# Writing out the attention heads' loop, and storing split weights in longer rows

## What is computed

```python
x = L0_attn_x                                   # (1, 1024, 256)
xn = layernorm(x)
s = attention(xn, wq, wk, wv, wo, ...)          # 16 heads of 128; q and k are RMS-normed
g = silu(mixture_of_experts_0(xn, ...))         # 32 experts of width 128
x = x + s * g
xn = layernorm(x)
s = gated_linear_attention(xn, Wq, ..., W1, W3, W2)   # a recurrence, then a gated MLP
g = silu(mixture_of_experts_1(xn, ...))         # 64 experts of width 64
x = x + s * g
```

## Time and profile before

| | |
|---|---|
| Median of 3 runs | 1166.0 us (1164.7 to 1166.66) |
| Span of the profiled execution | 1166.5 us |
| PE (TensorE matmuls) busy | 1036.1 us, 89% |
| VectorE busy | 827.8 us, 71% |
| ScalarE busy | 622.8 us, 53% |
| POOL busy | 579.7 us, 50% |
| DMA packets | 196552, 122.42 MB |

### The profile page before, as it was taken

How to read it: one execution, slowest core, us unless ns; L and a number is a source line. 1 busy time by engine, 2 the same in 40 slices (tenths; PEclk the granted TensorE clock), 3 DMA queues, 4 the chain that set the end, 5 groups by cost and what they waited for, 6 DMA issues and landing times. The chain is left out here.

```text
span 1166.5 us, 23260 instructions
## 1 busy us (share of the span) xinstructions
PE 1036.1 (89%) x7790; PEld 689.9 (59%) x7790; DVE 827.8 (71%) x1461; ACT 622.8 (53%) x1225; POOL 579.7 (50%) x449
## 2 busy tenths in 40 slices
PE   5976979999999999699999999979987967979797
PEld 4465766666666666366666666647933425557544
DVE  3768347877887688478787778854569974866557
ACT  3555166667666666366666666742360115646532
POOL 3211557657765776366586556443218401631173
PEclk9965999999999999899999999989998989979899
DMA  5664023757674755736755765563011308659932
GB/s 173 113 198 133 1 55 64 63 102 81 97 64 101 76 96 70 103 41 84 86 89 82 79 96 74 73 94 110 1 68 77 126 12 253 209 164 299 309 91 90
DMA packets 196552, 122.42 MB, mean 105 GB/s; under 512 B 75044, under 2 KB 189782, under 8 KB 196182
## 3 DMA queue, kind: packets, MB, share of 16 engines
q1 hardware_dynamic: 178934, 97.74, 45.7%
q10 hardware_dynamic: 14432, 14.81, 3.8%
q0 software_dynamic: 3072, 8.39, 2.1%
HBM read 81.90 MB, written 36.37 MB: 101 GB/s over the span
## 5 line engine op out<-in xcount | busy, mean ns | idle before, releaser
L1309 DVE TENSOR_REDUCE a_nmax<-psum 128x1 f32<-128x1024 f32 x128 | 156.1, 1219 | 83.7 <-PE psum L1157 79.2
L1315 DVE SCALAR_TENSOR_TENSOR a_pT<-psum,a_pT 128x512 f16<-128x512 f32 x256 | 164.9, 684 | 25.9 <-ACT a_pT L1252 19.2
L1252 ACT ACTIVATE a_pT<-psum 128x512 f16<-128x512 f32 x256 | 140.4, 603 | 25.7 <-PE psum L1168 14.1
L1070 POOL TENSOR_TENSOR a_rnorm<-a_ss,a_power 128x8 f32<-128x8 f32 x32 | 58.4, 1824 | 182.0 <-DVE a_ss L1285 182.0
L1244 ACT ACTIVATE a_ex<-psum,a_nmax 128x1024 f32<-128x1024 f32 x128 | 142.6, 1114 | 11.4 <-PE psum L1168 10.6
L1168 PE MATMUL psum<-ident,a_ex 128*128 128x128 f32 x1024 | 134.4, 274 | 8.2 <-issue 7.9
L1168 PEld LDWEIGHTS psum<-ident,a_ex 128*128 128x128 f32 x1024 | 120.2, 141 | 26.5 <-DVE a_pT L1315 1.7
L1139 PE MATMUL psum<-a_wh,xT_h 128*128 128x128 f16 (+1 forms) x512 | 115.2, 248 | 2.0 <-PEq L2754 2.0
L1140 PE MATMUL psum<-a_wl,xT_h 128*128 128x128 f16 (+1 forms) x512 | 115.2, 248 | 0.0
L1141 PE MATMUL psum<-a_wh,xT_l 128*128 128x128 f16 (+1 forms) x512 | 115.0, 248 | 0.0
L1179 PE MATMUL psum<-a_pT,a_vh 128*128 128x512 f16 x256 | 98.1, 383 | 12.0 <-DVE a_of L988 11.0
(11 more groups left out here) (397 smaller groups left out, 2536.0 us busy)
## 6 DMA issues: line engine op xcount, KB each, us to landing
split_gate_up<-a_e_wh SPq DMA_DIRECT2D x64, 128.0 KB
a_rb<-row_scales SPq DMA_DIRECT2D x32, 256.0 KB, 4.0
g_e_gu<-split_gate_up SPq DMA_DIRECT2D x32, 256.0 KB, 3.7
block_outputs<-g_e_ym ACTq DMA_DIRECT2D x16, 512.0 KB, 4.9
split_rest<-a_e_wh SPq DMA_DIRECT2D x45, 128.0 KB
wf<-in_L_ffn_W_gate SPq DMA_DIRECT2D x32, 128.0 KB, 2.4
wf<-in_L_ffn_W_up SPq DMA_DIRECT2D x32, 128.0 KB, 2.5
wf<-in_L_ffn_W_down SPq DMA_DIRECT2D x32, 128.0 KB, 3.0
```

What stands on the lines that cost most here:

```text
L1252: act.activation(pT[g][:, 0, 4 * h:4 * h + 4, (m % 4) * P:(m % 4 + 1) * P], bank_of(r, unit).rearrange("p (k q) -> p k q", k=4), ACT.Copy, ...
L1309: dve.tensor_reduce(nmax[:, k:k + 1], score_banks(m), AX.X, ALU.max, negate=True).then_inc(max_ready, 1)
L1315: dve.scalar_tensor_tensor(low, bank_of(r, unit).rearrange("p (k q) -> p k q", k=4), PROB, high, ALU.mult, ALU.subtract).then_inc(low_done, 1)
```

## The change

- `heads` has no loop any more: all 16 heads are written out on TensorE, ScalarE and VectorE, and POOL's list is written out as well. The same instructions on tiles are issued in the same order; what a wait compares with is now a constant.
- In POOL's split the halves' buffer of an expert chunk is laid out as (block of 256 numbers, half, 256), so that high and low of a block lie side by side: 1 KB. The two instructions that write it (L822, L826) and the one between them (L824) have three-dimensional views. For the chunks of the rest the layout stays.
- `store` issues two DMAs for a chunk, not three: for expert chunks one with gate and up (256 rows of 1 KB) and one with down (128 rows of 1 KB), for the rest one for each half (128 rows of 1.5 KB each). Counts of the semaphore `stored` go from 48 to 32 a chunk. What lies in DRAM afterwards is the same as before, and so are its readers.

```diff
-        self.halves = [tmp(f"e1_wh{b}", [P, 2, self.WIDTH], F16) for b in range(2)]
+        halves = [tmp(f"e1_wh{b}", [P, 2 * self.WIDTH], F16) for b in range(2)]
+        self.blocks = [x[:, :].rearrange("p (i a d) -> p i a d", a=2, d=D) for x in halves]
+        self.parts = [x[:, :].rearrange("p (a c) -> p a c", a=2) for x in halves]
...
-        whole = self.wf[b][:, :]
-        lift = self.lift.to_broadcast([P, self.WIDTH])
-        high, low = self.halves[b][:, 0, :], self.halves[b][:, 1, :]
+        t, j = k // 3, k % 3
+        if j < 2:
+            whole = self.wf[b][:, :].rearrange("p (i d) -> p i d", d=D)
+            lift = self.lift.unsqueeze(2).to_broadcast([P, self.WIDTH // D, D])
+            high, low = (self.blocks[b][:, :, part, :] for part in range(2))
+        else:
+            whole = self.wf[b][:, :]
+            lift = self.lift.to_broadcast([P, self.WIDTH])
+            high, low = (self.parts[b][:, part, :] for part in range(2))
         pool.wait_ge(self.loaded[b], 16 * self.LOADS * uses)
-        if not (isinstance(uses, int) and uses == 1):
-            pool.wait_ge(self.stored[b], 48 * uses - 48)
+        if uses > 1:
+            pool.wait_ge(self.stored[b], 32 * uses - 32)
...
             two = slice(4 * t + 2 * j, 4 * t + 2 * j + 2)
+            sp.dma_start(self.gu[two, :, :, :].rearrange("e p a x -> p e (a x)"),
+                         self.blocks[b][:, 0:2, :, :].rearrange("p e a x -> p e (a x)")).then_inc(self.stored[b], 16)
+            sp.dma_start(self.dn[two, :, :, :].rearrange("e f a d -> (e f) (a d)"),
+                         self.blocks[b][:, 2, :, :].rearrange("p a d -> p (a d)")).then_inc(self.stored[b], 16)
+        else:
             for part in range(2):
-                sp.dma_start(self.gu[two, :, part, :].rearrange("e p x -> p e x"),
-                             self.halves[b][:, part, 0:2 * self.GU].rearrange("p (e x) -> p e x", e=2)).then_inc(self.stored[b], 16)
-            sp.dma_start(self.dn[two, :, :, :].rearrange("e f a d -> (e f) a d"), self.halves[b][:, :, 2 * self.GU:])\
-              .then_inc(self.stored[b], 16)
-        else:
-            for at in range(0, self.WIDTH, D):
-                sp.dma_start(self.rest[:, :, t * self.WIDTH + at:t * self.WIDTH + at + D], self.halves[b][:, :, at:at + D])\
+                sp.dma_start(self.rest[:, part, t * self.WIDTH:(t + 1) * self.WIDTH], self.parts[b][:, part, :])\
                   .then_inc(self.stored[b], 16)
...
-        def heads(engine, head):
-
-            head(0, 0)
-            head(1, 1)
-            with engine.Fori(0, 2) as i:
-                for r in range(2, 8):
-                    head(6 * i + r, r)
-            head(H - 2, H - 2)
-            head(H - 1, H - 1)
+        def heads(head):
+            for t in range(H):
+                head(t, t)
...
-                for t in range(2):
-                    past(t, 1 - t, t + 2, t % 2, 3 * t // 2 + 1)
-                with pool.Fori(0, (H - 6) // 2) as i:
-                    for b in range(2):
-                        past(2 * i + 2 + b, 1 - b, i + 3 + b, b, 3 * i + 4 + b)
-                for t in range(H - 4, H):
-                    past(t, 1, H // 2, t % 2, 3 * t // 2 + 1)
+                for t in range(H):
+                    past(t, (t + 3) % 2, (t + 3) // 2 + 1, t % 2, 3 * t // 2 + 1)
```

More of the change, by code:

```diff
@@ L851, in wait_stored @@
         for b, done in enumerate(self.stored):
-            sp.wait_ge(done, 48 * len(range(b, chunks, 2)))
+            sp.wait_ge(done, 32 * len(range(b, chunks, 2)))
 def attention0(nc, env, w):
@@ L1202, in _ @@
                 scores(0, 1, 0, None)
-                heads(pe, head)
+                heads(head)
                 for piece in range(4):
@@ L1271, in _ @@
                 exps(0, 0)
-                heads(act, head)
+                heads(head)
                 high_outputs(act, H - 1, 0)
@@ L1356, in _ @@
                 squares(1, 0, NS + 2)
-                heads(dve, head)
+                heads(head)
                 finished(dve, H - 1, 0)
```

## The result

| | before | after |
|---|---|---|
| Median (runs) | 1165.35 us (4: 1163.7 to 1166.66) | 1147.68 us (4: 1142.63 to 1151.09) |
| Ratio, 95% interval | | 0.9848, 0.9821 to 0.9875 |
| Span of the profiled execution | 1166.5 us | 1146.6 us |
| DMA packets | 196552 | 175819 |

The forecast was 1147.9 us. That it came so close is partly luck, as the account by stages shows: three terms were too small, and other stages and the step from the span to the median took their excess back.

A forecast was written before the change was run, and what follows sets the result against it. PE was taken as the bound, busy 89% of the span. The jump's 13.4 and register work's 4.7 us, 18.1 together, off the 1166.5 us span gave 1148.4, less 0.5 for the median 1147.9 us; range 1138 to 1154.

The forecast's parts named there:

- The jump: Head 8, where the loop jumps back: writing it out removes idle time and the low clock after it, 13.4 us.
- Rival (4): Stall at 480 to 489 us is DMA's and returns: about 1161 or 1166; 0.02 with no gain, 0.03 shared with one stop.
- the case of one new stop: Written-out list fetched late once, at the jump's price of 13.4 us: 1161.3; 0.03, shared with the DMA stall keeping part gain.
- The register work: Loop's heads: working out wait values in registers costs 0.39 us a head, for 12 heads 4.7 us, ends 2.0 and 8.8.
- the middle of 0.17 and 0.60: Register cost a head taken as 0.39 us, between the L1126 wait difference and all idle time above head 1's.
- POOL's split and the longer rows: POOL's three-dimensional views and SP's fewer stores in longer rows were taken to be worth nothing to PE.
- The stop in head 15 stays: Row load (14, 1) stays caught behind the slow row store; PE's 6.91 us idle remains, no gain counted.
- the limit of 769.4: Head 15's row load must issue by 769.4, 1.85 us earlier, but its earlier row store lands only then.
- Rival (1): The stop in head 15 goes too, giving back at most 7.6 us: 1140.3; chance 0.34.
- the last step of the sum: From span to median: the runs' median lies 0.5 below the span, so 1148.4 becomes 1147.9 us.
- Rival (3): Written-out list fetched late in heads 8 to 13, 13.4 us each time: 1174.7 from the second stop on, chance 0.04.
- Rival (2): Only the jump counts; the loop heads' 1.03 us idle has other causes: 1152.6, at worst 1155.6; chance 0.15.

The follow-up runs named there:

- hold_all: Kernel before, with SP's row store (7, 1), store of chunk 23 and load of chunk 25 held back until TensorE passed the jump; 1166.08 us in one run.
- loop_rows16: Kernel before, loop and weight stores kept, with row sums stored as 128 rows of 16 bytes and VectorE's strided read; 1149.02 us, ratio 0.9798.
- heads_out: Kernel before with only the loops written out on all four engines, stores still three a chunk in rows of 512 bytes; 1144.33 us, ratio 0.9861.
- after_third: The changed kernel unedited, measured a third time, on another chip; 1160.84 us, ratio 0.9888 to the kernel before.
- long_rows: Kernel before with the new longer-row stores and POOL's list written out; TensorE, ScalarE and VectorE keep their loop; 1162.89 us, ratio 1.0016.
- after_again: The changed kernel unedited, measured and profiled once more; 1144.84 us, ratio 0.9871 to the kernel before.
- hold_chunks: Kernel before, with SP's store of chunk 23 and load of chunk 25 held back until TensorE's first scores behind the jump; 1168.89 us in one run.
- hint_loop: Kernel before, with an instruction per loop turn announcing the jump back to the instruction fetch on TensorE, ScalarE and VectorE; 1171.06 us, ratio 1.0047.
- no_jump: Kernel before, its loop of two turns made two loops of one turn; register work vanished too on TensorE, ScalarE and VectorE; 1145.79 us, ratio 0.9878.
- rows16: The changed kernel with inverse row sums stored as 128 rows of 16 bytes, not 512 numbers of 4, and VectorE's strided read; 1143.57 us, ratio 0.9795.
- rows16_last: The changed kernel with 16-byte row stores and VectorE's strided read in heads 14 and 15 alone; 1153.55 us, ratio 0.9831.

## Why the prediction was right, step by step

**The jump, 13.4 us: right, and the reason was half of it.** Head 8 lost 14.2 us, of which 0.6 are its share of the next term. Idle time and the clock's fall went together, as said: behind PE's single idle time of 7.90 us the clock falls, and in head 8 of hold_all and loop_rows16, where PE's longest is 1.88 and 1.49 us, it stays at 1.00. Behind PE's 3.64 us in the changed kernel's head 15 it falls too (0.96 over the head). The Trainium skill, "Runtime: NRT & Kernel Launch", Instruction fetch mechanics, says that a taken branch to a place outside what has been fetched forces a fetch by DMA before execution can go on. The trace agrees: the stop of 10.92 us stands behind the jump and goes when the jump is announced. What the prediction missed is that other DMA traffic sets the length of that fetch. Rival (4) held the stall for DMA's and gave it, together with the case of one new stop, 5 in 100; it was wrong that the stall would come again, but right that DMA has a hand in it: 7.3 to 7.7 of 10.9 us are the row store's (3.61 us are left in loop_rows16, 3.18 in hold_all). Written out, the same place has no stop although the same row store runs beside it (heads_out).

**The register work, 4.7 us (ends 2.0 and 8.8): the size held, the cause did not.** By length, heads 2 to 13 went from 38.93 to (230.30 + 38.20 + 192.00) / 12 = 38.38 us, which is 0.55 a head and 6.7 us in all. Of this only 0.18 a head, 2.2 us, is register work, and that is just what the two waits at L1126 had shown, 0.52 against 0.35, the lower end. The step that failed is the one from there to the middle of 0.17 and 0.60: heads 1 and 14 idle for 0.43 and 0.42, which was read as the loop's doing, while most of the rest was waits that come and go with the 4-byte stores, in or out of a loop. Another execution could have given another size for this term: in after_third the heads idle for 1.40 us, more than before's 1.03, though on a chip where before is slower too.

**POOL's split and the longer rows, nothing: right.** The split's first instruction takes 1467 ns as before:

```profile
L830 POOL TENSOR_TENSOR a_e_wh<-a_e_wf,a_lifts x47: 1457/1467/1475, 183.1 to 752.0; 128x768 f16<-128x768 f32 x47
```

and long_rows is at 1.0016. The Trainium skill, "DMA: Bandwidth & Descriptors", Specifications, has 512 bytes as the size from which DMA runs at line rate and says that transfers below it are read, changed and written back. The first half shows here: from 512 to 1536 bytes nothing is gained (1.0016). The second can't be the whole reason for what the 4-byte stores do, since the 16-byte rows are below 512 bytes too and land in 1.4 us. The prediction used the first half and passed over small rows altogether, though the row store's 9.7 us to landing stood in its own rows.

**The stop in head 15 stays: wrong for this execution.** It gave 3.9 us, and it was called near even. The step that failed is the limit of 769.4: it took the load as needing 4.0 us and the wait for the earlier row store as binding. In both kernels the load goes out as soon as SP's issue before it ends (768.21 + 2.93 = 771.14 before, 748.48 + 1.69 = 750.17 after), so SP's overlong issues set its time. In the changed kernel the load went 1.7 us earlier relative to VectorE, not the 1.85 asked for, VectorE itself came a little later (754.82 - 740.44 = 14.4 us behind the half before, where 13.7 would have done), and the next row store followed after 3.5 us, not 1.03. That is a margin of parts of a microsecond, and the runs show both sides: no stop in after, after_again (but 2.3 to 2.6 us at the next half), a stop of 6.97 us in heads_out, 7.59 in after_third and 7.73 in hold_chunks, 3.66 in long_rows, 1.31 in hint_loop, 2.06 and 2.27 in no_jump. Rival (1)'s price of at most 7.6 us had its reason right, that the next row load has to wait for its store: that load is what was late in after.

**What was in no term.** Head 0 took 1.7 us less, by its clock. It takes 34.3 us in ten of the executions and 32.6 in four (after, heads_out, hold_all, rows16), so it doesn't follow the change. Layer 1 took 4.5 us more, and what stands ahead of head 0 and heads 1 and 14 together 1.3. So the close hit is a sum: 2.0 for the heads, 3.9 for head 15 and 1.7 for head 0 were missed on one side, 4.5 and 1.3 on the other. That leaves 1.8 us, the span falling by 19.9 where 18.1 were forecast. They were taken back by the last step of the sum, that the median is 0.5 below the span: after, it is 1.1 above (1147.68 against 1146.6). Each run's time is some 1.9 us over its own span, and by that the profiled execution of before took longer than the median of its kernel.

Rival (3) fell: no head of the written-out list has a stop, in any of the runs. Rival (2)'s time fell too, but its reason held for most of the idle time: 0.18 of 0.60 us a head is register work, and the rest has other causes.

**What stays open.** How a store of 512 numbers of 4 bytes holds up a fetch or a load that isn't behind it in its queue was not tried. The edit to 16-byte rows changes three things at once, the size of a piece (4 to 16 bytes), their number (512 to 128) and their order in DRAM (neighbouring numbers came from different partitions); which of them counts was not separated. That the misleading announcement makes hint_loop's second stop was not separated. rows16 was not measured beside the changed kernel. That it is faster rests on its ratio, 0.9795 (0.9766 to 0.9825) against 0.9848 (0.9821 to 0.9875), 0.9871 and 0.9888, and on loop_rows16 and rows16_last, which beat the changed kernel beside them. How much it gains depends on how many waits the changed kernel meets: from head 0's first exponentials to the end of head 15, rows16 takes 605.0 us, the changed kernel 607.3 and 607.7 in two executions and 626.0 in after_third.

## What to carry to other kernels

Before unrolling a loop, price two things apart: the jump, from the first head behind it, and the register work, from the smallest difference at a wait that both forms have. Where a short transfer lands late again and again (some 10 us for 2 KB here), look at the size of its rows before its place in the queue: storing 16 bytes in a row in place of 4 was worth more than writing out the loop where the two were measured beside each other (0.9798 against 0.9888), since most of the stop at the jump goes with it. A gain that hangs on a margin of a microsecond between two transfers is a coin's throw; with the cause of the late transfer taken away, head 15 was without its stop in all four executions. And before a close forecast is called understood, compare stage by stage, with more than one profile of each kernel: here stages that the change doesn't touch move by up to 8 us from one execution to another.

## What was not expected of the hardware

- A DMA store of 128 x 4 numbers of 4 bytes, each to a place of its own, lands in 7 to 11 us; in rows of 16 bytes the same 2 KB land in 1.4 us in the median, 5.6 at most. In kernels with the first, code fetches and 256 KB row loads can be late, and SP's issues take up to 6.4 us (5.48 for a pair in head 15 that takes 1.27 elsewhere).
- A code fetch behind a jump stops VectorE for 3.2 to 3.6 us with no such store under way (hold_all, loop_rows16), and 10.5 to 10.9 with one (long_rows, hold_chunks, before).
- An announced jump costs next to nothing (0.86 us idle in head 8, VectorE's wait behind the jump 0.93), but in a loop of two turns the exit then costs 11.8 us of idle time.
- VectorE takes 1.09 us in place of 0.68 for 128 x 512 numbers when one of its operands, in 4-byte numbers, is read in steps of 16 bytes.
